# Graph network kernel: adjacency tiles of the first stage handled by halves, one half between two projected row tiles

## The reference, cut to what matters

```python
g = (h @ W_lin.T).reshape(n, 8, 32)
el = jnp.einsum('nhd,d->nh', g, a_l)
er = jnp.einsum('nhd,d->nh', g, a_r)
e = el[:, None, :] + er[None, :, :]
e = jnp.where(e >= 0, e, 0.2 * e)
a = softmax(where(adj == 0, -inf, e), axis=1)
out = jnp.einsum('ijh,jhf->ihf', a, g)
```

## Time and profile before

| | |
|---|---|
| median of 3 runs | 2209.24 us (2208.99 to 2215.06) |
| profiled execution, its own time | 2210.15 us |
| its span | 2208.4 us |
| PE busy | 1979.8 us (90%) |
| DVE busy | 1877.9 us (85%) |
| ACT busy | 1607.4 us (73%) |
| POOL busy | 914.7 us (41%) |
| end of the first stage (first matmul of the next) | 175.75 us |

### The profile page before, as it was taken

One profiled execution on the slowest core, in us unless ns is written; L12 is line 12 of the kernel. 1 busy time (PEld: TensorE's weight loads), 2 busy tenths in 40 slices (PEclk: granted clock), 3 DMA queues, 4 the chain that ended last, 5 costly groups with the idle time before them and its releaser, 6 DMA issues. The chain is left out here.

```text
span 2208.4 us, 58755 instructions
## 1 busy us (share of the span) xinstructions
PE 1979.8 (90%) x23674; PEld 1552.3 (70%) x23674; DVE 1877.9 (85%) x4155; ACT 1607.4 (73%) x1914; POOL 914.7 (41%) x952
## 2 busy tenths in 40 slices
PE   4748999999995899999887999999999999977999
PEld 4548999999994788888654666666666666655544
DVE  5587999999997899988668999999999999985222
ACT  4557999999994776552266999999999999885100
POOL 0020000000005434446316888888888888860000
PEclk9958999999998899999898999999999999997999
DMA  9798221221201156679564212222122211101222
GB/s 306 288 367 308 75 90 57 75 89 55 95 22 41 54 147 160 156 164 190 124 177 144 71 38 69 71 71 70 37 71 71 71 65 42 40 7 48 81 81 71
DMA packets 178078, 235.13 MB, mean 106 GB/s; under 512 B 112195, under 2 KB 143971, under 8 KB 174481
## 3 DMA queue, kind: packets, MB, share of 16 engines
q1 hardware_dynamic: 153408, 203.68, 30.1%
q10 hardware_dynamic: 24400, 27.70, 3.8%
HBM read 161.79 MB, written 49.00 MB: 95 GB/s over the span
## 5 line engine op out<-in xcount | busy, mean ns | idle before, releaser
L2200 DVE CUSTOM_DVE_ANT_0 h_S<-h_ps,off 128x832 f32<-128x832 f32 x832 | 800.1, 1019 | 17.4 <-PE h_ps L2099 16.3
L2099 PE MATMUL h_ps<-KS,QS 98*128 98x416 f16 x1664 | 441.5, 347 | 74.4 <-DVE h_mx L2200 43.0
L2159 ACT ACTIVATE h_H<-h_S,h_nmx 128x2048 fp8e4<-128x2048 f32 x208 | 416.7, 2003 | 69.7 <-DVE h_nmx L2206 69.7
L844 ACT ACTIVATE b_CA<-room,HC 128x1152 fp8e4<-128x1152 f32 (+1 forms) x384 | 435.5, 1219 | 0.0
L945 PE MATMUL b_pb<-xb,room 128*128 128x132 f16 x5408 | 415.8, 222 | 3.6 <-DVE room L906 3.2
L945 PEld LDWEIGHTS b_pb<-xb,room 128*128 128x128 fp8e4 x5408 | 341.9, 97 | 6.5 <-DVE room L906 6.0
L2053 POOL TENSOR_SCALAR h_gap<-h_S,h_nmx 128x1280 f32<-128x1280 f32 x208 | 277.1, 1332 | 91.2 <-DVE h_nmx L2206 81.6
L2058 POOL TENSOR_SCALAR h_H<-h_gap 128x1280 uint8<-128x1280 f32 x208 | 260.5, 1253 | 17.2
L926 PE MATMUL b_pz<-xb,adjT 128*128 128x134 f16 x2704 | 258.1, 222 | 4.3 <-PEq L306 4.3
L2130 PEld LDWEIGHTS h_po<-Vhl,h_HT 128*128 128x128 fp8e4 x5408 | 214.8, 98 | 64.9 <-ACT h_HT L2166 0.7
L2099 PEld LDWEIGHTS h_ps<-KS,QS 98*128 98x128 f16 x1664 | 95.8, 97 | 192.9 <-DVE h_mx L2200 119.0
(11 more groups left out here) (246 smaller groups left out, 3192.0 us busy)
## 6 DMA issues: line engine op xcount, KB each, us to landing
h_rows<-in_adj_dram SPq DMA_DIRECT2D x24, 1663.5 KB, 7.4
room<-in_adj_dram SPq DMA_DIRECT2D x25, 832.0 KB, 6.6
room<-in_adj_dram SPq DMA_DIRECT2D x25, 831.5 KB, 7.5
e_dram<-c_U ACTq DMA_DIRECT2D x78, 256.0 KB, 3.1
xb<-xv_dram SPq DMA_DIRECT2D x44, 435.5 KB, 5.1
adjT_dram<-adjT SPq DMA_DIRECT2D x1, 10816.0 KB, 32.2
c_ad<-adjT_dram SPq DMA_DIRECT2D x13, 832.0 KB, 6.8
m_ad<-adjT_dram SPq DMA_DIRECT2D x13, 832.0 KB, 4.5
```

The costliest lines, as they stand in the source:

```text
L844: nc.scalar.activation(dst[:, 0:cols], elr[:, n % 2, 0:cols], ACT.Sigmoid, bias=HC[:, h, 1, jt:jt + 1], scale=STEP, saturate=False).then_i ...
L2099: last = nc.tensor.matmul(ps[:, ch % 2, b, 0:SB], QS[:, i % 2, h, :], KS[:, h, c0:c0 + SB], start=True, stop=True)
L2159: nc.scalar.activation(H[:, g % 2, 0:CA], S[:, g % 2, 0:CA], ACT.Exp, bias=nmx[:, g % 2:g % 2 + 1], scale=1.0, saturate=False).then_inc(s_ ...
L2200: nc.vector.tensor_tensor_reduce(out=two(S[:, g % 2, ch * SW:(ch + 1) * SW]), in0=ps[:, ch % 2, :, 0:SB], in1=two(off[:, i % 2, ch * SW:(c ...
```

## The change

`startup_order()` gives halves instead of whole tiles: an "adj" step is now (a, f), and SP, TensorE, ScalarE and VectorE do only the half f. Steps are dealt out differently, too. Before, a projection group had one or two whole tiles in it, and the 16 factors had 11. Now one half follows the turn, each projected tile and "left", so a group has six halves; 24 tiles stand ahead of scale and two are dealt out among the first factors.

```diff
 def startup_order():
 
-    order = [("adj", 0), ("weights", 0), ("adj", 1), ("adj", 2)]
-    a = 3
+    halves = [("adj", (a, f)) for a in range(NT) for f in range(2)]
+    take = lambda n: [halves.pop(0) for _ in range(min(n, len(halves)))]
+    order = take(2) + [("weights", 0)] + take(4)
     for g in range(NGROUPS + 1):
         if g < NGROUPS:
             order.append(("turn", g))
-        order.append(("adj", a))
+        order += take(1)
         if g:
-            order += [("project", t) for t in range(GROUP * (g - 1), min(GROUP * (g - 1) + 2, NT))]
-        if g % 2:
-            order.append(("adj", a + 1))
-        if g:
-            order += [("project", t) for t in range(GROUP * (g - 1) + 2, min(GROUP * g, NT))]
-            order.append(("left", g - 1))
-        a += 1 + g % 2
+            for t in range(GROUP * (g - 1), min(GROUP * g, NT)):
+                order += [("project", t)] + take(1)
+            order += [("left", g - 1)] + take(1)
+        else:
+            order += take(1)
     order.append(("scale", 0))
-    rest = NT - a
     for n in range(len(FACTORS)):
-        while a < NT and (a - (NT - rest)) * len(FACTORS) <= n * rest:
-            order.append(("adj", a))
-            a += 1
-        order.append(("factor", n))
-    return order + [("adj", x) for x in range(a, NT)]
+        order += [("factor", n)] + take(1)
+    return order + halves
...
             for kind, i in order:
-                if kind == "adj" and i + 2 < NT:
-                    load(i + 2)
+                if kind == "adj" and i[0] + 2 < NT:
+                    load(i[0] + 2, i[1])
...
                 if kind == "adj":
-                    act.wait_ge(s_atr[1], i + 1)
-                    nc.scalar.activation(k.adjT[:, TILES_IN[i], HALF:NT, :].rearrange("p j i -> p (j i)").bitcast(U8),
-                                         tr[:, 1, 0:HC1].bitcast(U16), ACT.Copy, scale=float(FP8_ONE)).then_inc(s_aev[1], 1)
+                    a, f = i
+                    if f == 1:
+                        act.wait_ge(s_atr[1], a + 1)
+                        nc.scalar.activation(k.adjT[:, TILES_IN[a], HALF:NT, :].rearrange("p j i -> p (j i)").bitcast(U8),
+                                             tr[:, 1, 0:HC1].bitcast(U16), ACT.Copy, scale=float(FP8_ONE)).then_inc(s_aev[1], 1)
```

More of the change, by code:

```diff
@@ L340, in _, with load @@
         def _(sp):
-            def load(a):
+            def load(a, f):
                 s, t = a % 2, TILES_IN[a]
[L343 to L348, removed]
+                c0, c1 = f * HC1, (N if f else HC1)
+                if a >= 2:
+                    sp.wait_ge(s_atr[f], a - 1)
+                for p0, p1 in (LAST_CUTS if t == NT - 1 else ((0, P),)):
+                    sp.dma_start(rows[p0:p1, s, c0:c1], adj_dram[t * P + p0:t * P + p1, c0:c1]).then_inc(s_rows[s][f], 16)
             for (t0, t1), done in zip(halves, (s_xa, s_xb)):
@@ L357, in _ @@
             sp.wait_ge(s_corner, 1)
-            load(0)
-            load(1)
+            for a in range(2):
+                for f in range(2):
+                    load(a, f)
             for kind, i in order:
-                if kind == "adj" and i + 2 < NT:
-                    load(i + 2)
+                if kind == "adj" and i[0] + 2 < NT:
+                    load(i[0] + 2, i[1])
             for f in range(2):
@@ L400, in _, with transposes @@
         def _(pe):
-            def transposes(a):
-                t = TILES_IN[a]
+            def transposes(a, f):
                 if a == 0:
                     pe.wait_ge(s_id, 3)
[L405 to L414, removed]
+                landed(pe, a, f)
+                if a == 2 and f == 1:
+                    pe.wait_ge(s_pad, 3)
+                if a:
+                    pe.wait_ge(s_aev[f], a)
+                for n in range(HALF):
+                    j0 = (f * HALF + n) * P
+                    last = nc.tensor.transpose(tr[:, f, n * P:(n + 1) * P], low16[:, a % 2, j0:j0 + P, 0], k.ident16[:])
+                last.then_inc(s_atr[f], 1)
             def weights():
@@ L466, in _ @@
                 if kind == "adj":
-                    transposes(i)
+                    transposes(*i)
                 elif kind == "weights":
@@ L664, in _ @@
                 if kind == "adj":
-                    dve.wait_ge(s_atr[0], i + 1)
-                    nc.vector.tensor_scalar(k.adjT[:, TILES_IN[i], 0:HALF, :].rearrange("p j i -> p (j i)").bitcast(U8),
-                                            tr[:, 0, 0:HC1].bitcast(U16), float(FP8_ONE), None, ALU.mult).then_inc(s_aev[0], 1)
+                    a, f = i
+                    if f == 0:
+                        dve.wait_ge(s_atr[0], a + 1)
+                        nc.vector.tensor_scalar(k.adjT[:, TILES_IN[a], 0:HALF, :].rearrange("p j i -> p (j i)").bitcast(U8),
+                                                tr[:, 0, 0:HC1].bitcast(U16), float(FP8_ONE), None, ALU.mult).then_inc(s_aev[0], 1)
                 elif kind == "weights":
```

## The result

| | before | after |
|---|---|---|
| median | 2211.57 us (2208.65 to 2216.54, 20 runs) | 2215.99 us (2211.72 to 2219.95, 20 runs) |
| ratio to before | | 1.0018, 95% interval 1.0011 to 1.0025 |
| span of the profiled execution | 2208.4 us | 2216.5 us |
| first matmul of the next stage | 175.75 us | 182.40 us |
| from there to the end of the span | 2032.7 us | 2034.1 us |

The change costs 0.18%, some 4 us: within the 0.3% that I had called "same". The time is 5.5 us above the forecast of 2210.5 and inside the range, whose end was 2220. But 2.3 us of these 5.5 are the kernel before, whose median was 2209.24 in the three runs that I forecast from and is 2211.57 in twenty: as a difference of medians, +1.3 us was forecast and +4.4 was measured.

The account below looks back on a forecast made before the run. The first stage was taken as bound by a chain of engines in the projections, then by DMA traffic in the factor loop. +21.1 - 19.9 = +1.2 us gave a median of 2210.5 us, range 2200.5 to 2220.

Parts of the forecast that it names:

- the bounds given (170 to 184): First stage's end: the forecast counts as wrong if it falls before 170 or after 184 us.
- Step 1: Start of the first stage, up to TensorE's third turn: placed near 55 us instead of 53.0.
- Step 2: Projection groups: a chain sets 13.1 us from turn to turn, against 12.2 for the DMA; last turn near 107 us.
- T: Time of a group's turn on TensorE; VectorE's adjacency copy was forecast done 7.2 us after it.
- the seven pieces: TensorE's serial work after that copy: four half-tile transposes, two projections and "left", 5.9 us.
- E: When TensorE ends the transposes of tile 23 ahead of scale: 126 us, between 122.5 and 129.
- Step 3: From tile 23's transposes to the first factor: 10.3 us, inputs ready at 136.3 us, 21.1 us later than before.
- Step 4: Factor loop: 39.8 us instead of 59.7, a gain of 19.9 us; a pair of factors costs 4.5 us.
- Sum: Whole change: +21.1 us ahead of the factor loop, -19.9 in it, so +1.2 us.
- Rival A: Factor loop: VectorE and POOL don't take turns, a pair costs 2.9 us, time 2200.9; chance 0.14.
- Rival B: Projection groups: loads issued in bursts land after 8.9 us instead of 4.7, +13 us, 2223; chance 0.10.
- Rival C: Projections: TensorE drops to the lower clock, +5 us a group, +20 us, 2231; chance 0.06.

Follow-up runs that it names:

- the best dealing: Changed kernel with 17.5 tiles ahead of scale instead of 24, next group's ReLUs spread over projected tiles, products still shared by VectorE and POOL: 2197.04 us, ratio 0.9935.

## Why the prediction was right, and where it was wrong

The verdict alone says little, since any sum within 6.6 us of nothing would have given it. What speaks for the working is that its two parts of about 20 us each came out 4.9 us (inputs ready) and 0.6 us (loop) from their forecasts.

- *Verdict and range.* Right: 0.18% is within "same", and 2215.99 within the range. The profiled stage end, 182.40 us, lies inside the bounds given (170 to 184), near the upper one, and all later stages together moved by 1.4 us.
- *Step 1, start.* The third turn is at 56.0 us, forecast 55: +1.0.
- *Step 2, the groups: the term that was mis-sized.* The turns are 14.8, 13.4, 13.4 and 14.2 us apart, where 13.1 three times and 12.2 were forecast: +4.2. The mechanism was right. TensorE goes on at T+7.45 (78.25 - 70.80; forecast T+7.2), and the seven pieces took 84.16 - 78.25 = 5.9 us, as forecast. What was missing are two things beside it. In the group at 56.02 the pieces behind the wait of 3.54 us ran at the lower clock at first (1.2 GHz; 0.50 is the granted clock from 63.5 to 66 us; 1.54 and 1.60 us instead of 0.89 and 0.88), 7.3 us in all instead of 5.9. In the group at 97.52 the five waits for loads add up to 3.7 us, the longest 1.98, where the DMA's pace that I had taken leaves such a group 12.2 - 9.8 = 2.4. The last turn came at 111.7 instead of 107 (the working's 106.5, rounded up), and with 1.4 us more behind it E was **132.1 instead of 126**, past even the 129 that I had given as its upper bound. That bound assumed a longer chain in every group, and not a chain and a DMA wait one after the other.
- *Step 3, from E to the first factor.* 141.2 - 132.1 = 9.1 us, forecast 10.3: the last store to el_dram was issued at once, not 1.2 us later. Inputs ready 26.0 us later than before, forecast 21.1.
- *Step 4, the loop.* 40.4 us, forecast 39.8: right in the whole and in the pair (4.36 and 4.5). The start took 0.9 us more than forecast (12.6 and 11.7), since POOL's first product came 5.5 us behind its inputs and not 4.8. The experiment with all products on VectorE shows that the cause is the one named.
- *Sum in these terms.* 26.0 - 19.3 = +6.7 us at the stage's end, which is what the trace shows; +1.2 was forecast: +4.9 ahead of the loop and +0.6 in it. The medians differ by 4.4 us.
- *Rival A* (no taking of turns) is excluded: the subtractions' mean is 1.64 us, not 1.05. *Rival B* (bursts land late) shows itself once, mildly: the load issued at 95.50 us took 9.1 us, and cost TensorE 1.98. *Rival C* (lower clock) is excluded as a lasting state: PEclk is 0.96 and 1.00 over the projections. As a passing one it cost 1.4 us, behind the wait of 3.54 us. The Trainium skill, page "TensorE: Matmul & The Clock Gate", section "HAM oscillation — how this bites in real kernels", has pieces of matmul work that are shorter than the wait for the next load start cold each time. The trace of the changed kernel disagrees behind the wait of 2.90 us, which is longer than the 1.6 us of work ahead of it and behind which the pieces ran at full clock (0.89 at 78.25), and agrees once, behind the wait of 3.54 us. The length of the last wait does not settle it, though: with tiles in one piece the granted clock fell behind a wait of 2.67 us, and only when TensorE had been at work again for over 1 us (90.65).
- *What the prediction did not see.* It treated the edit as one and gave splitting no term of its own, and alone it makes the kernel 0.3% faster. Had splitting been priced, for instance by the wait of 2.69 us for VectorE's bank, the better kernel (halves, dealt out as of old) could have been named beforehand. Nor did it see that POOL's late first product, which it kept as a fixed 4.8 us, is tied to the all-reduce that stands ahead of it on POOL (last section).

## What to carry to other kernels

When an edit both cuts work finer and deals it out differently, price the two apart: here one gained 3 us at the stage's end and the other lost 10, and the sum hid a kernel that is 0.3% faster with the old dealing (and 0.4% with one between, which is not clear of the 0.3%). If DMA traffic is to be moved to a stretch where it idles, move only as much as leaves it busy in both: the share by stretch (0.77 and 0.92 before, 0.97 and 0.44 after, 0.97 and 0.89 in the best dealing) shows on which side traffic is missing. It is a rough guide: halves with the old dealing have 0.91 and 0.90, and their stage still ends 9.1 us later than the best one's. The GB/s beside the shares tell them apart better (321 and 357 against 369 and 337, and 336 against 353 over the stage from 20 us to its end). And POOL, where it "helped" VectorE with a two-input operation, cost it nearly as much time as it took itself (1.5 of 1.68 us), unless its work lay beside the copy that reads PSUM.

## What the runs showed of the hardware that was not expected

**POOL is held up behind a partition all-reduce.** Where an instruction was ready by then, it started 7.1 to 8.2 us after its end (7.21 in the earlier trace rows, 7.94, 7.62 and 8.23 above, 7.07 in halves with the old dealing), even a product of 128 x 8 elements with its inputs long there. Where nothing came for 540 us, the next one still started 4 us behind its inputs, in another layer, and 4.4 us of the whole kernel's time hung on it (2199.96 us and 2195.56 us, with one tiny instruction between them). So a part of the delay falls due only when the next instruction comes. Long idleness is not the cause: behind the tiny product H started 0.1 us after its inputs, 544 us later. What POOL does in that time the trace does not show, and no run leaves the all-reduce out, so that it is the cause is argued from its place in every trace. The Trainium skill, page "GPSIMD Engine Reference", section "2.1 Instruction dispatch", has the first call of a freshly loaded kernel pay about 6 us for loading code, with no instruction in the profile for it. The size is near and nothing else here bears it out: the gap stands behind the all-reduce, ahead of an ordinary product. That it is code that is fetched back is a guess, and no run tested it.
